# A four-layer decoder on one core: spreading the reciprocal deviations of every layer norm by fp32 transposes in place of fp32 matmuls

## What is computed

```python
def _layernorm(x, axis=-1, eps=1e-05):
    m = jnp.mean(x, axis=axis, keepdims=True)
    v = jnp.var(x, axis=axis, keepdims=True)
    return (x - m) / jnp.sqrt(v + eps)

x = x + _L0_attn_ref(_layernorm(x, axis=-1), ...)
x = x + _L0_xattn_ref(_layernorm(x, axis=-1), ctx_1024, ...)
x = x + _L0_ffn_ref(_layernorm(x, axis=-1), ...)
...
x = x + _L3_ffn_ref(_layernorm(x, axis=-1), ...)
```

## The kernel before, in words

| norm | stage | first spread, us | TensorE's order around the spreads |
|---|---|---|---|
| 1 | `begin`, before linear attention | 12.8 | `norm_pe`, a block of its own |
| 2 | `project` for L0's context attention | 187.5 | key, spread, variance, query units in turn |
| 3 | `experts` | 457.1 | `norm_pe` with `follow` (the gate's logits) |
| 4 | `batch_attention` | 651.4 | `norm_pe` with `follow` (projections) |
| 5 | `layer_norm`, before `wide_head_attention` | 734.6 | `norm_pe`, a block of its own |
| 6 | `token_shift_ffn` | 808.3 | `norm_pe` |
| 7 | `shift_attention` | 836.4 | `norm_pe` with `follow` (projections) |
| 8 | `project` for L2's context attention | 943.1 | as 2 |
| 9 | `quantised_ffn` | 1187.5 | `norm_pe` |
| 10 | `project` for L3's self-attention | 1245.9 | query and key from `xn` |
| 11 | `project` for L3's context attention | 1407.3 | as 2, with 256 keys, and a gate behind |
| 12 | `lora_ffn` | 1566.9 | `norm_pe` with `follow` (first products) |

## Time and profile before

### The profile page before, as it was taken

One profiled execution on the slowest core, in us unless ns is written; L12 is line 12 of the kernel. 1 busy time (PEld: TensorE's weight loads), 2 busy tenths in 40 slices (PEclk: granted clock), 3 DMA queues, 4 the chain that ended last, 5 costly groups with the idle time before them and its releaser, 6 DMA issues. The chain is left out here.

```text
span 1617.8 us, 30013 instructions
## 1 busy us (share of the span) xinstructions
PE 1439.9 (89%) x10746; PEld 725.6 (45%) x10746; DVE 992.2 (61%) x1940; ACT 804.3 (50%) x1498; POOL 455.9 (28%) x656
## 2 busy tenths in 40 slices
PE   7998899999999999878987899899977788978887
PEld 5777634444454443536653452222334333433354
DVE  5666488888163221364557759998376667356746
ACT  4455437677633332304541054777754456445647
POOL 7111220000003567240035430000021456134531
PEclk9999999999999999979997899999986989898999
DMA  2000263221110000001000055322000431143100
GB/s 102 1 0 0 98 203 100 54 51 30 52 69 1 1 0 0 1 1 46 18 7 1 0 161 169 100 54 50 20 13 9 167 100 50 37 167 101 51 2 27
DMA packets 82393, 85.45 MB, mean 53 GB/s; under 512 B 7244, under 2 KB 67916, under 8 KB 81772
## 3 DMA queue, kind: packets, MB, share of 16 engines
q1 hardware_dynamic: 82296, 84.18, 16.9%
HBM read 51.06 MB, written 32.51 MB: 52 GB/s over the span
## 5 line engine op out<-in xcount | busy, mean ns | idle before, releaser
L1335 ACT ACTIVATE arena<-ps 128x1024 f32<-128x1024 f32 x256 | 261.8, 1023 | 109.4 <-PE ps L1242 108.9
L1227 PE MATMUL ps<-k_stack,q_stack 49*128 49x512 bf16 x512 | 190.6, 382 | 14.5 <-DVE small L1358 12.1
L1242 PE MATMUL ps<-q_stack,k_stack 51*128 51x256 bf16 x1024 | 189.6, 272 | 0.6 <-ACT arena L1335 0.4
L1355 DVE CUSTOM_DVE_ANT_0 small<-ps,mask_b 128x512 bf16<-128x512 f32 x256 | 168.0, 689 | 29.6 <-PE ps L1227 28.1
L1358 DVE TENSOR_REDUCE small<-ps 128x1 f32<-128x512 f32 x256 | 162.0, 685 | 15.9 <-PE ps L1227 14.9
L1544 DVE TENSOR_REDUCE small<-ps 128x6 f32<-128x768 f32 x128 | 122.6, 958 | 76.3 <-PE ps L1424 73.8
L1254 PE MATMUL ps<-arena,v_pad 128*32 128x256 f32 x2048 | 162.4, 391 | 1.1 <-ACT arena L1335 1.1
L1521 ACT ACTIVATE arena<-ps 128x384 f32<-128x384 f32 x256 | 118.0, 488 | 78.4 <-PE ps L1446 77.7
L1132 POOL TENSOR_SCALAR_AFFINE_SELECT arena<-arena 128x256 f32<-128x256 f32 x256 | 101.8, 406 | 86.6 <-ACT arena L1521 86.3
L2602 DVE TENSOR_TENSOR arena<-ps,arena 128x512 f32<-128x512 f32 x64 | 44.3, 692 | 101.1 <-PE ps L2519 101.0
L2676 POOL TENSOR_TENSOR arena<-arena 128x512 f32<-128x512 f32 x64 | 79.7, 1266 | 94.3 <-ACT arena L2571 94.3
(11 more groups left out here) (357 smaller groups left out, 2983.7 us busy)
## 6 DMA issues: line engine op xcount, KB each, us to landing
q_stack<-q_scratch SPq DMA_DIRECT2D x128, 96.0 KB
k_stack<-k_scratch SPq DMA_DIRECT2D x64, 192.0 KB
k_scratch<-arena SPq DMA_DIRECT2D x8, 768.0 KB, 3.9
k_stack<-k_scratch SPq DMA_DIRECT2D x64, 96.0 KB
q_scratch<-arena SPq DMA_DIRECT2D x4, 1152.0 KB, 7.5
arena<-in_ctxT SPq DMA_DIRECT2D x8, 512.0 KB, 6.3
k_scratch<-arena SPq DMA_DIRECT2D x8, 512.0 KB, 4.7
k_scratch<-arena SPq DMA_DIRECT2D x16, 256.0 KB, 3.8
```

Source lines behind the costliest of these rows:

```text
L1227: pe.matmul(ps[:, t, :], c.q_stack[par][64 * e:64 * e + ROW_MAX, pr, t * P:(t + 1) * P], c.k_stack[par][64 * e:64 * e + ROW_MAX, pr, :], s ...
L1242: mm = pe.matmul(ps[:, bank, (ch % 2) * S:(ch % 2 + 1) * S], c.k_stack[prv][64 * e:64 * e + ROWS, pr, ch * P:(ch + 1) * P], c.q_stack[prv] ...
L1335: act.activation(buf.probs[i % 8], ps[:, bank:bank + 2, :].rearrange("p a n -> p (a n)"), ACT.Exp, scale=scale).then_inc(g["probs"].sem, 1)
L1355: dve.tensor_tensor_reduce(buf.junk[t], ps[:, t, :], c.mask_b[:, M_X + t * SC:M_X + (t + 1) * SC], 1.0, FLOOR, op0=ALU.add, op1=ALU.max, a ...
```

## The change

In `norm_spread` the call of `c_matmul` becomes a call of `pe.transpose` with the same three operands: the same PSUM columns, the same broadcast column as the stationary operand, the same identity as the moving operand.

```diff
 def norm_spread(c, pe, rstd, out):
     for j in range(4):
-        mm = c_matmul(pe, out[:, j * P:(j + 1) * P], rstd[:, j:j + 1].to_broadcast([P, P]), c.ident[:, :])
+        mm = pe.transpose(out[:, j * P:(j + 1) * P], rstd[:, j:j + 1].to_broadcast([P, P]), c.ident[:, :])
     return mm
```

## The result

| | before | changed |
|---|---|---|
| median of 20 runs | 1627.06 us | 1615.03 us |
| lowest and highest | 1614.77 to 1636.96 | 1607.86 to 1634.91 |
| span of the profiled execution | 1617.8 us | 1607.8 us |
| TensorE busy | 1439.9 us | 1424.4 us |
| time at a TensorE clock of 1.2 GHz within that span | 150.2 us | 177.5 us |

The ratio is 0.9941, with a 95% interval of 0.992 to 0.9962, so the change takes off 9.6 us (6 to 13). The forecast was 14.45 us less than before and a time of 1617.4 us. The time lies well within its range. About a third of the forecast difference did not arrive, and that did not show in the time, because the median of the first three runs before, 1631.9 us, stood some 5 us above that of all twenty.

A forecast was written before the change was run, and what follows sets the result against it. TensorE, busy for 89% of the span, was taken as the bound. Of 21.6 us saved there, the norms' terms summed to 14.45 us reaching the end, taking the median from 1631.9 to 1617.4 us; range 1612 to 1623.

The forecast's parts named there:

- The price of a spread and of four transposes: On TensorE, a spread of four fp32 matmuls takes 0.89 us, four transposes 0.44; each of 48 spreads saves 0.45 us.
- rival D: In all spreads, transposes are cheaper still, 0.22 us a spread: 21.5 us saved, 1610.4 us; chance 0.04.
- rival E: In all spreads, the broadcast fp32 column still goes in two passes, so nothing changes: 1631.9 us; chance 0.03.
- Norms 1 and 5: After variance 3, VectorE's order of scales binds, so 1.1 of TensorE's 1.8 us reach each block's end: together 2.2 us.
- Norms 3, 4, 6, 7, 9 and 12: Only spreads that hold up later work count: 1.8, 0.9, 0.9, 0.9, 0.1 and 1.8 us less.
- Norms 2 and 8: TensorE runs without waits through to the attention's first scores, so all four spreads count: 1.8 us each, together 3.6 us.
- it still fits, narrowly: Behind norms 2 and 8, the stacks' last load lands by 209.4 when moved, before the scores would start at 209.9.
- Rival A: Transfers take more back: stacks bind in norms 2 and 8, 0.9 us each; total 12.2 us, 1619.7 us; chance 0.12.
- Norm 10: The attention waits for its stacks, whose second part stands behind three spreads; three count, the fourth lengthens the wait: 1.35 us.
- Norm 11: TensorE is 1.8 us earlier, but its wait for the row maxima grows to some 1.6 us: 0.9 us saved.
- Rival C: Less TensorE work makes the clock fall to 1.2 GHz behind each of twelve norms, costing 18.7 us: 1636.1 us; chance 0.03.
- its milder case: The clock falls to 1.2 GHz four times, 6.2 us given back: 1623.7 us; chance 0.05.

The follow-up runs named there:

- the doubled transposes: The changed kernel with every transpose issued twice, so a spread holds TensorE for 8 passes as before the change: ratio to before 0.9977, 1625.29 us.
- the pair with extra matmuls: Unused bf16 matmuls ahead of spreads in norms 1, 4, 5, 6, 7, 9, 10, 12: added to the change 1615.79 us, to the kernel before 1631.43 us.
- one transpose in four: The changed kernel with only the first of each spread's four transposes issued, output incomplete: ratio to before 0.992, 1614.46 us.
- the first kernel with both kinds: The changed kernel with fp32 matmuls kept in norms 1, 5, 6 and 9 and transposes in the rest: ratio to before 0.9975, 1624.13 us.

## Why the prediction was right or wrong

**The price of a spread and of four transposes.** One pass in place of two was right, and rival D is out: by the factor of 4 that the Trainium skill states ("TensorE: Matmul & The Clock Gate", its table of terms) a spread would have given 0.67 us, and rival E would have kept 384 records. The saving was mis-sized by a tenth: 0.50 us, so that four transposes hold TensorE for about 0.39 us where I took 0.44. The error was to choose the pace of the variances' surroundings over that of L534's transposes (0.41); the lower bound was the nearer.

**Norms 1 and 5.** VectorE's order binds, as the step says: in norm 5 the three scales follow one another, and it gave 1.2 us (forecast 1.1). In norm 1 the fall of the clock, 9.5 us behind its start, turned 1.1 us into -0.4. That norm 5's stage became shorter by 2.2 us owes 1.0 us to something else: before, the clock fell again at the stage's end (69.4 us behind the norm's start), and after it did not. With the doubled transposes, where that fall is missing too, the stage took 71.8 us (73.7 before), with a norm of 11.3.

**Norms 3, 4, 6, 7, 9 and 12.** 1.9, 1.0, 1.0, 1.0, 0.3 and 2.0 us, against 1.8, 0.9, 0.9, 0.9, 0.1 and 1.8: the counts of spreads (four, two, two, two, none, four) were right, and most of the rest is the price. In norms 3, 4, 7 and 12 the stage behind the norm was shorter by another amount (3.5, 0.4, 0.0, 0.2 us). The 3.5 us behind norm 3 are partly chance: with the norm at 13.9 us each time, its stage took 195.2, 196.9 and 196.9 us in the three profiled repetitions of the change. Before, the clock fell for 3.4 us there, behind the norm, and after it did not. In the stages of norms 7 and 12 it was the other way: more time at 1.2 GHz after than before (37.5 against 34.1 us, and 13.7 against 6.8). For norm 4, with 20.5 us on both sides, I did not find out where the remainder of 0.5 us went.

**Norms 2 and 8.** The norms gave 1.7 and 1.15 us. Behind norm 2 the attention waits 1.43 us for its stacks, which the step "it still fits, narrowly" denied. What failed is its premise that the landing of the stores moves along. The first of the six stores was issued 1.2 us earlier behind the norm's start (16.2 us, 17.4 before), but the first load, which follows when the last of them has landed, came 9.0 us behind that, 7.4 before; so the loads begin no earlier than before. In the three repetitions of the change that distance was 7.8, 7.4 and 8.9 us, and the wait 0.5, 0.4 and 1.1 us. I had put no spread on a transfer's time. Rival A, in part, is what happened in norm 2; in norm 8 the profiled repetitions took 19.7, 19.9 and 21.7 us, so that its saving was 1.2 to 1.4 us in two and none in the third, where the clock fell 6.1 us behind its start; which of its four spreads was hidden was not tried.

**Norm 10.** The wait for the stacks came out at 3.38 us, forecast 3.3. But the norm grew by 1.1 us, because the clock was at 1.2 GHz for 8.3 us of it (3.1 us before). In the three repetitions too it fell within norm 10, 9.5 to 11.5 us behind its start, and the norm took 21.3 to 23.3 us.

**Norm 11.** 1.5 us in place of 0.9 (2.3 with its stage). The step that failed is that the transfer of the row maxima "stands directly behind a queue of 24 loads", so that the queue decides when it starts. The waits of SyncE's queue before the change, at the end of these loads, show what it waited for:

```profile
SPq L1063 <- ACT max_rows L1169: 0.2, 1, 0.2
```

The queue was free 0.2 us before ScalarE had the maxima ready, and these come from TensorE's own scores; so the transfer moves with TensorE. After, the stores were issued 0.9 us earlier, as the step says, and landed 1.4 us sooner as well, so the loads began 2.3 us earlier. In the three repetitions the queue then waited 0.9 to 1.6 us for the maxima, and TensorE's wait was 0.66 us, as before. In the profile of the changed kernel one load's issue took 1.50 us in place of 0.44, the maxima stood directly behind the loads after all, and the wait was 0.77 us. Nowhere was it 1.6.

**The clock.** This is where most of the expected gain went that did not arrive. At an equal clock the change is worth 14.8 us (the pair with extra matmuls, with 9 to 20 us as its bounds), and my sum with the measured price would be 14.45 x 0.50 / 0.45 = 16.1 us; measured are 9.3 us. By these, some 5 to 7 us are given back; the size is uncertain, since the pair's lower bound lies near the 9.3 us themselves. That the clock takes something is not: across the runs of one kernel the time grows by 0.35 us for each us at 1.2 GHz (time and mean granted clock of every run, 99 of before and 49 of the change; the slopes are 0.345 and 0.348), and the median run of the change has some 31 us more of it. That would be 11 us, more than is missing. Either the slope does not hold for these falls, many of which come when TensorE is about to rest anyway, or more of the spreads' time than in my sum reaches the end; no run decides this.

Rival C had the mechanism and its milder case nearly the size (6.2 us given back), and I gave this case 0.05. The step that failed is the argument against it, "TensorE has only some 0.45 us less to do between two variances, and most norms run straight into more matmuls"; the sign that I had named for being wrong, "if the clock falls where it was 1.00", came in norms 1, 5, 6 and 9. A norm is three such spaces in a row, not one, and half of a spread's passes was enough to tip it in 35 of 45 cases where eight passes tipped it in 3 of 21. My price per fall, 1.56 us, lies between what single norms show: 1.0 us in norm 4 (18.4 us with a fall, 17.4 without), 2.7 us in norm 12 (15.1 or 15.2 against 12.5), and nearly nothing in norm 5 (10.3 against 10.2).

**The base.** I set the median 14.1 us above a span. A run's time is only 1.7 us above its own span (1609.51 us for the profiled run of 1607.8). The other 12.4 us were the distance of a short execution from the median of three longer ones. Had I used 1.7 us, the forecast would have been 1605 us, 10 us below the measured median and below the range that I gave. The good agreement of 1617.4 with 1615.0 us is therefore in part luck: the gain was too large by 5 us, and the base too.

## What to carry to other kernels

An fp32 operand that is only to be spread or turned cost TensorE one pass as a transpose and two as a matmul here, and where TensorE bound, the saved half was paid out nearly in full within the norm. Before counting it, mark the blocks that are made of many short matmuls, as these norms are, and look in several profiles whether their clock holds: taking work out of them can cost the clock, and the gain then stops growing, as it did with one transpose in four. Compare a forecast with the profiled execution's own time; the median of three runs stood 12 us (0.8%) above it here, nearly as much as the change was to give.

## What the runs showed of the hardware

- An fp32 matmul of 128 columns against a 128x128 operand leaves two records, a transpose of the same operands one. Eight passes of either kind take the same time (the nine norms named with the doubled transposes, as long as before within 0.3 us).
- The executions of one kernel on one core differ by some 20 to 30 us (1607.86 to 1634.91 for the first 20 of the change), and their mean granted clock explains nearly all of it: about the line through time and time at 1.2 GHz they scatter by 1.9 us, for the change as for before.
- The clock can fall while TensorE shows no idle time: in norm 12 with transposes (the first kernel with both kinds) the trace shows it busy without a gap from the norm's first mean through the fall, 8.6 us behind it.
